# Routing weights of the first expert layer: spread by DMA from DRAM in fp32 instead of by a matmul of bf16 parts

## The reference

```python
scores = sigmoid(x @ gate_w.T)                      # 64 experts
rw = weights of the 8 chosen experts per token, 0 for all others   # [T, 64], fp32
expert_out = vmap(lambda gw, uw, dw: silu(x @ gw.T) * (x @ uw.T) @ dw.T)(Wg, Wu, Wd)
routed = einsum('eth,te->th', expert_out, rw)
shared = silu(x @ Sg.T) * (x @ Su.T) @ Sd.T
out = routed + shared
```

## Time and profile before

| | us |
|---|---|
| median of 3 runs (1984.31 to 1989.08) | 1984.51 |
| the profiled execution, whole time | 1989.54 |
| its span | 1987.7 |
| `setup` and `attention`, to about | 383 |
| `route0`, to | 493.7 |
| `block0`, from DVE's first L1594 to its last | 1014.4 |
| `block1` and the output, from 1509.6 | 478 |

### The profile page before, as it was taken

One profiled execution on the slowest core, in us unless ns is written; L12 is line 12 of the kernel. 1 busy time (PEld: TensorE's weight loads), 2 busy tenths in 40 slices (PEclk: granted clock), 3 DMA queues, 4 the chain that ended last, 5 costly groups with the idle time before them and its releaser, 6 DMA issues. The chain is left out here.

```text
span 1987.7 us, 25546 instructions
## 1 busy us (share of the span) xinstructions
PE 1782.0 (90%) x7668; PEld 1062.7 (53%) x7668; DVE 1425.5 (72%) x2688; ACT 809.7 (41%) x1501; POOL 677.8 (34%) x610
## 2 busy tenths in 40 slices
PE   2888898652999999999899899998998999999999
PEld 1455555351666656656566565565664455555555
DVE  5777777378666786986979969779699487444444
ACT  1466667532333324334343233342434443443333
POOL 2011111100000681945828638368194275000000
PEclk9989889855999999999999999999999999999999
DMA  7544444010223353333333333333330000000000
GB/s 267 151 134 111 120 119 115 23 51 13 104 106 111 101 178 94 99 90 97 89 95 98 87 95 95 90 100 85 95 101 11 1 6 6 6 6 5 6 5 5
DMA packets 101065, 157.68 MB, mean 79 GB/s; under 512 B 11077, under 2 KB 49310, under 8 KB 97785
## 3 DMA queue, kind: packets, MB, share of 16 engines
q1 hardware_dynamic: 97351, 154.61, 26.1%
q10 hardware_dynamic: 1586, 1.30, 0.2%
q0 software_dynamic: 2048, 0.79, 0.2%
HBM read 123.23 MB, written 33.42 MB: 79 GB/s over the span
## 5 line engine op out<-in xcount | busy, mean ns | idle before, releaser
L1296 PE MATMUL psum<-e_hhi,e_ring 128*128 128x512 f32 x704 | 478.2, 679 | 37.5 <-DVE e_hm L1737 26.2
L1551 ACT ACTIVATE e_gu<-psum 128x512 f32<-128x512 f32 (+1 forms) x368 | 219.1, 597 | 627.8 <-PE psum L1298 510.5
L1305 PE MATMUL psum<-e_hm,w_d 128*128 128x512 f32 (+1 forms) x736 | 378.6, 597 | 1.1 <-DVE e_hm L1733 1.1
L1733 DVE TENSOR_TENSOR e_gu<-psum,e_gu 128x512 f32<-128x512 f32 x352 | 240.9, 684 | 174.2 <-PE psum L1335 158.6
L1801 POOL TENSOR_TENSOR e_prod<-e_state,e_phi 128x512 f32<-128x512 f32 x256 | 355.3, 1424 | 5.5 <-DVE e_y L1608 3.2
L1769 DVE TENSOR_TENSOR e_hm<-psum,e_gu 128x512 f32<-128x512 f32 x256 | 175.2, 689 | 203.7 <-ACT e_gu L1576 152.0
L1297 PE MATMUL psum<-e_hhi,e_ring 128*128 128x512 f32 x704 | 281.2, 399 | 0.0
L1298 PE MATMUL psum<-e_hlo,e_ring 128*128 128x512 f32 x704 | 280.5, 399 | 0.0
L1415 PE MATMUL psum<-e_hm,w_gu 128*128 128x512 f32 x512 | 264.0, 601 | 3.2 <-DVE w_d L1751 2.6
L1576 ACT ACTIVATE e_gu<-psum 128x512 f32<-128x512 f32 x256 | 152.4, 597 | 279.0 <-PE psum L1298 264.8
L1737 DVE TENSOR_TENSOR e_hm<-psum,e_gu 128x512 f32<-128x512 f32 x352 | 243.5, 692 | 12.1
(11 more groups left out here) (237 smaller groups left out, 2404.7 us busy)
## 6 DMA issues: line engine op xcount, KB each, us to landing
e_ring<-w_split SPq DMA_DIRECT2D x308, 256.0 KB, 2.6
qk_parts<-at_part SPq DMA_DIRECT2D x96, 192.0 KB, 2.9
w_split<-e_ring SPq DMA_DIRECT2D x44, 256.0 KB, 2.0
at_qs<-qk_parts SPq DMA_DIRECT2D x16, 576.0 KB
at_ks<-qk_parts SPq DMA_DIRECT2D x16, 576.0 KB
w_gu<-in_w SPq DMA_DIRECT2D x2, 2048.0 KB, 10.4
sel_buf_r<-w_split SPq DMA_DIRECT2D x14, 256.0 KB, 2.6
w_gu<-in_wg SPq DMA_DIRECT2D x1, 2904.0 KB
```

Of the source, the lines that this page charges most:

```text
L1296: pe.matmul(out, w_hi, x_hi, start=first, stop=False)
L1305: mm = pe.matmul(ps[:, ACC, :], weights_at(T, WD + P * j, P)[0:rows(j), :], hm[0:rows(j), slot(j), :], start=(j == 0), stop=(j == HT - 1))
L1551: a(act_g[0:r, j % 2, :], ps[0:r, GB[j % 2], :], ACT.Silu).then_inc(silu_done, 1)
L1733: ins = v.tensor_tensor(product, ps[0:r, UB[j % 2], :], act_g[0:r, j % 2, :], ALU.mult)
```

## The change

`route0` no longer cuts the weights into bf16 parts. PE transposes `w1` itself in fp32 (32 transposes, 4 for each chunk), ACT and DVE copy 64 x 512 values for even and odd chunks, and SP writes them to a DRAM tensor `rw_dram` of 64 x 4096. All of it waits for these 8 writes.

In `block0` the spreading matmul and `sel` are gone. SP loads the weights of a tile's rows into one of four slots `rb` in SBUF: one DMA per expert that owns rows in the tile, with the expert's row of 2 KB read once for each hidden row (2 or 3 DMAs per tile, 104 per chunk). DVE multiplies up by the slot into bank RB, which is in PSUM, and then that by the silu. Only the second of these waits for the silu.

```diff
@@ route0: the parts
-            dve.wait_ge(weighted, 2)
-            for u in range(2):
-                dve.wait_ge(upper_cut, u + 1)
-                v.tensor_tensor(half(w0, u), half(w1, u), part(0, u), ALU.subtract).then_inc(rest_ready, 1)
...
-            with dve.Fori(0, CHUNKS // 2) as i:
-                keep(2 * i, 0)
-                keep(2 * i + 1, 1)
+            for c in range(1, CHUNKS, 2):
                 dve.wait_ge(tr_done, c + 1)
-                v.tensor_copy(T["rw"][0:PARTS * EHALF, 1, ds(c * CHUNK, CHUNK)], ps[0:PARTS * EHALF, 3 + 2 * (k % 2), :])\
-                    .then_inc(tr_kept[1], 1)
+                v.tensor_copy(cols(rw_fm, c)[0:EXPERTS], ps[0:EXPERTS, 2 + c % 4, :]).then_inc(tr_kept[1], 1)
@@ route0: PE
+            for c in range(CHUNKS):
+                pe.wait_ge(weighted, 1 + c // (CHUNKS // 2))
+                if c >= 4:
+
+                    pe.wait_ge(tr_kept[c % 2], c // 2 - 1)
+                for t in range(CT):
+                    mm = pe.transpose(ps[0:EXPERTS, 2 + c % 4, t * P:(t + 1) * P], w1[:, (CT * c + t) * EXPERTS:(CT * c + t + 1) * EXPERTS],
+                                      T["ident"][:])
                 mm.then_inc(tr_done, 1)
@@ route0: SP
+            for c in range(CHUNKS):
+                sp.wait_ge(tr_kept[c % 2], c // 2 + 1)
+                sp.dma_start(cols(T["rw_dram"], c), cols(rw_fm, c)[0:EXPERTS]).then_inc(rw_out, 16)
+            sp.wait_ge(rw_out, 16 * CHUNKS)
@@ experts: SP
+            def load_rb(c, j):
+
+                if j >= ROUTED_TILES:
+                    return
+                if c > 0 or j >= RB_SLOTS:
+                    sp.wait_ge(gu_done, ROUTED_TILES * c + j - RB_SLOTS + 1)
+                s = j % RB_SLOTS
+                for first, last, e in owners(j):
+                    sp.dma_start(rb[first:last, s, :], T["rw_dram"][e:e + 1, c * CHUNK:(c + 1) * CHUNK].broadcast_to([last - first, CHUNK]))\
+                        .then_inc(rb_in[s], 16)
...
                     sp.dma_start(w_slots[slot_of(j)].bitcast(F32), split[j]).then_inc(split_in[slot_of(j)], 16)
+                    load_rb(c, j)
@@ experts: PE
-                if j < ROUTED_TILES:
-                    mm = pe.matmul(ps[:, RB[j % 2], :], sel[0:PARTS * EHALF, j % HALF_TILES, :],
-                                   rw[0:PARTS * EHALF, j // HALF_TILES, ds(c * CHUNK, CHUNK)], start=True, stop=True)
                 mm.then_inc(ur_done, 1)
@@ experts: DVE
-                    dve.wait_ge(silu_done, g + 1)
                     dve.wait_ge(ur_done, g + 1)
-                    product = gu[0:r, j % 2, :] if j < ROUTED_TILES else hm[0:r, slot(j), :]
-                    ins = v.tensor_tensor(product, ps[0:r, UB[j % 2], :], act_g[0:r, j % 2, :], ALU.mult)
                     if j < ROUTED_TILES:
-                        ins.then_inc(gu_done, 1)
+                        s = j % RB_SLOTS
+                        dve.wait_ge(rb_in[s], 16 * rb_loads(s, ROUTED_TILES) * c + 16 * rb_loads(s, j + 1))
+                        v.tensor_tensor(ps[:, RB[j % 2], :], ps[0:r, UB[j % 2], :], rb[:, s, :], ALU.mult).then_inc(gu_done, 1)
+                        dve.wait_ge(silu_done, g + 1)
                         dve.wait_ge(gu_done, ROUTED_TILES * c + j + 1)
-                        v.tensor_tensor(hm[:, slot(j), :], ps[:, RB[j % 2], :], gu[:, j % 2, :], ALU.mult).then_inc(hm_done, 1)
+                        v.tensor_tensor(hm[:, slot(j), :], ps[:, RB[j % 2], :], act_g[:, j % 2, :], ALU.mult).then_inc(hm_done, 1)
```

More of the change, by code:

```diff
@@ L878, in _ @@
             run(pe, step_)
-            pe.wait_ge(cut, 1)
-            pe.wait_ge(T["ffn0_loaded"], 16 * FFN0_LOADS)
-            def turn(c, k):
-                if k >= 2:
-                    for g in range(2):
-                        pe.wait_ge(tr_kept[g], c - 1)
-                for g in range(2):
-                    for t in range(CT):
-                        mm = pe.matmul(ps[0:PARTS * EHALF, 2 + 2 * (k % 2) + g, t * P:(t + 1) * P],
-                                       parts[:, ds(CT * c + t, 1), g, :, :].rearrange("p o i e -> p (o i e)"), T["ident_bf"][:],
-                                       start=True, stop=True)
-                mm.then_inc(tr_done, 1)
-            turn(0, 0)
-            turn(1, 1)
-            pe.wait_ge(cut, 2)
-            with pe.Fori(1, CHUNKS // 2) as i:
-                turn(2 * i, 2)
-                turn(2 * i + 1, 3)
+            for c in range(CHUNKS):
[5 more added lines that the diff above has]
+                                      T["ident"][:])
+                mm.then_inc(tr_done, 1)
         @block.scalar
@@ L921, in _ @@
                 nc.scalar.activation(lg[:, over(u)], lg[:, over(u)], ACT.Sigmoid).then_inc(scored, 1)
-            for u in range(2):
-                act.wait_ge(weighted, u + 1)
-                nc.scalar.activation(part(0, u), half(w1, u), ACT.Copy).then_inc(upper_cut, 1)
-            for u in range(2):
-                act.wait_ge(rest_ready, u + 1)
-                nc.scalar.activation(part(1, u), half(w0, u), ACT.Copy).then_inc(upper_cut, 1)
-            def keep(c, k):
-                act.wait_ge(tr_done, c + 1)
-                nc.scalar.activation(T["rw"][0:PARTS * EHALF, 0, ds(c * CHUNK, CHUNK)], ps[0:PARTS * EHALF, 2 + 2 * (k % 2), :], ACT.Copy)\
-                    .then_inc(tr_kept[0], 1)
-            with act.Fori(0, CHUNKS // 2) as i:
-                keep(2 * i, 0)
-                keep(2 * i + 1, 1)
+            for c in range(0, CHUNKS, 2):
+                act.wait_ge(tr_done, c + 1)
+                nc.scalar.activation(cols(rw_fm, c)[0:EXPERTS], ps[0:EXPERTS, 2 + c % 4, :], ACT.Copy).then_inc(tr_kept[0], 1)
         @block.vector
@@ L1046 @@
 EARLY_LOADS = ("wqkv", "wo", "wr", "b_r1", "sel1")
-FFN0_LOADS = len(EARLY_LOADS) + 5
+FFN0_LOADS = len(EARLY_LOADS) + 4
 ROUTER_STEPS = 20
@@ L1057, with owners, rb_loads @@
 W_SLOTS = 5
+RB_SLOTS = 4
+def owners(j):
+    rows = range(P * j, P * (j + 1))
+    return [(max(HIDDEN * e, rows[0]) - rows[0], min(HIDDEN * (e + 1), rows[-1] + 1) - rows[0], e)
+            for e in range(rows[0] // HIDDEN, rows[-1] // HIDDEN + 1)]
+def rb_loads(slot, j):
+    return sum(len(owners(i)) for i in range(j) if i % RB_SLOTS == slot)
 def slot_of(j):
@@ L1145, in experts @@
         g1 = rw[:, 0, :]
+        rb = rw[:, 1, :].bitcast(F32).rearrange("p (s c) -> p s c", c=CHUNK)
         GB, UB, RB, ACC, SIDE = (0, 1), (2, 3), (4, 5), 6, 7
@@ L1190, in experts @@
         split_in = [sem(f"split_in{s}") for s in range(W_SLOTS)]
+        rb_in = [sem(f"rb_in{s}") for s in range(RB_SLOTS)]
         w1h_done, w1l_done = sem("w1h_done"), sem("w1l_done")
@@ L1274, in _ @@
                 sp.dma_start(split[j], w_slots[slot_of(j)].bitcast(F32)).then_inc(split_out[slot_of(j)], 16)
+                load_rb(0, j)
             for s in range(W_SLOTS):
@@ L1922, in layout @@
     a["wo"] = i["L1_attn_Wo"]
-    owner = (np.arange(HALF_TILES * P) // HIDDEN).reshape(HALF_TILES, P)
-    one_hot = (owner[None] == np.arange(EHALF)[:, None, None])
-    a["sel"] = f(np.tile(one_hot, (PARTS, 1, 1)).astype(bf16))
     a["wr"] = i["L1_ffn_router_w"]
```

27 lines of the change are left out of this document (6 added, 21 removed).

## The result

| | us | |
|---|---|---|
| before, median of 4 runs beside it | 1986.8 | 1984.3 to 1989.7 |
| after, median of 4 runs | 1958.9 | 1953.2 to 1963.6 |
| ratio | 0.9856 | 95% interval 0.9824 to 0.9889 |
| forecast | 1930 | 1913 to 1958 |

The change makes the kernel 1.4% faster: about 28 us, half of the 55 that I forecast, and 0.9 us outside my range. The profiled run of the changed kernel is its slowest (1963.63 us, span 1961.8); the spans differ by 25.9 us.

The account below looks back on a forecast made before the run. PE sets the pace in chunk 0 and up to tile 24 of late chunks, DVE behind it. Savings 6.8 + 10.2 + 7.5 + 30.6 = 55.1 us from 1989.5, less 5.0, give 1929.4, said as 1930; range 1913 to 1958.

Parts of the forecast that it names:

- The end of `route0`: Between the weights being ready and `experts`: fp32 transposes, last copy and store end earlier, saving 6.8 us.
- The spreading matmul's worth: In `block0`, each removed matmul frees 0.237 us where PE sets the pace; 22 count up to tile 24, giving 5.2.
- forecast 10.2: Chunk 0, where PE stays the bound: 43 x 0.237 = 10.2 us saved.
- The matmul in front of a projection: Tiles 12, 13 and 14 of chunks 2 to 7: removal gives nothing, and waits before the projections fall to about zero.
- Chunk 1: Chunk between the PE-bound and late ones: at least 5.2, at most 9.7 us saved, 7.5 taken.
- I take zero for all of it: Slot loads in `block0` cost nothing: DMA needs 1.86 of a tile's 2.26 us, and they are issued four tiles ahead.
- My forecast of a share of 0.67: Sign to look for in `block0`: DMA share near 0.67, no load waits on DVE or PE outside chunk 2's start.
- Same number, same kinds of input: DVE's multiplies in `block0`: the first, now writing PSUM, costs 0 to 0.31 us more; 0 taken.
- one drop per chunk: PE's clock in late chunks: one stretch at 0.57 for 4 us, after the 3.45 us wait before tile 43's up.
- a sign of failing: The prediction fails if PE's granted clock drops in more than one place of a chunk.
- My rival: TensorE loses its clock more often behind tile 24: up to 1.7 us per stretch, 24 in all, 1954; chance 0.10.

Follow-up runs that it names:

- experiment 12: Changed kernel with the silu wait before the first multiply, chunks 3 to 6 written out and only the first four slots loaded; 1928.3 us, ratio 0.9719.
- experiment 8: Changed kernel with the silu wait before the first multiply and chunks 3 to 6 written out; 1938.8 us, ratio 0.9751.
- experiment 7: Changed kernel with VectorE's silu wait moved from before the second multiply to before the first; 1948.9 us, ratio 0.9809.
- experiment 6: Changed kernel with only the first four slots loaded, plus a second, always satisfied wait before each first multiply; 1943.7 us.
- experiment 4: Changed kernel with a matmul of zeros on TensorE before the up matmuls of tiles 25 to 43 of chunks 2 to 7; 1961.0 us.
- experiment 1: Changed kernel with only the first four slots ever loaded, later tiles reading what stands in their slot; 1945.1 us, ratio 0.9779.

## Why the prediction was half right

- **The end of `route0`: right.** 6.8 forecast, 7.6 measured.
- **The spreading matmul's worth: right, with some luck.** From tile 23 on, the second multiplies of chunk 3 stand 5.2 to 5.5 us earlier than in chunk 5 before, where 22 x 0.237 = 5.2 was forecast. But 0.7 of it is there at tile 0 already, by the `e_hlo` multiply (0.69 us in place of 1.35); the matmuls gave about 4.6. In chunk 0 the run with the first four slots alone gained 10.5, forecast 10.2. The matmul in front of a projection did not quite vanish: the weight loads of three projections of chunk 3 wait 1.1 us in all, where I said zero, and the projections start 0.32 to 0.33 us behind the matmul ahead, where one stream takes 0.237.
- **Chunk 1: mis-sized.** I took 7.5 and called 5.2 the least. Without slot loads it gave 4.5 (5.1 in experiment 12), and no run says why.
- **"I take zero for all of it" (the slot loads): wrong, the first of the two steps that failed.** I had compared 1.86 us of DMA with 2.26 us of tile, and steady chunks bear that out. But chunks 0 and 1 are not steady. At the start of chunk 0 the slots' loads come with the first stores and nothing is ahead; at the start of chunk 1 five weight slots and the tiles' slots have to be filled at once, and an engine share of 0.80 leaves little to catch up with (that account is argued; the waits are in the rows above). Price by the chunks: 4.0 + 4.9 + 2.7 = 11.6 us, 10.8 between experiments 8 and 12; by the medians 1958.9 - 1945.1 = 13.8 and 1938.8 - 1928.3 = 10.5. My forecast of a share of 0.67 was near in chunks 2 to 7 (0.61 to 0.66); I never asked what it is in the chunks with the fastest tiles and the most to transfer, though the earlier trace rows had 0.29 and 0.41 there and the slot loads add some 0.4.
- **"Same number, same kinds of input" (VectorE's multiplies): wrong, the second.** Their time was right: the first took 693 ns on average after, 684 before. The Trainium skill, VectorE: DVE Perf Modes, first table, has VectorE closer to SBUF than to PSUM; on the output side this trace puts 9 ns on that at most, since the second multiply, which writes SBUF, takes 692 in both kernels. But I counted multiplies and not the semaphores that they wait for. In the written-out chunks the second multiply got a second one, 0.07 us on the path between two dependent instructions: 3.5 us of chunk 7 and 2.8 of chunk 2 (experiment 7), part of it in jobs that took longer behind it (experiment 8).
- **What I had no term for: the late start of chunks 4 to 6.** The three take 10.0 us more than three times chunk 3. 8.1 of them are there when the second multiply of tile 0 starts (7.33, 7.15 and 7.52 us into the chunk, 4.62 in chunk 3), 1.72 to 1.74 us behind a packet of instructions (experiment 6). Another 1.1 is lost in chunk 6 up to tile 10, most of it at the lower clock, and 0.8 at its end, also at the lower clock. Written out, the stall doesn't occur.
- **The clock: the count was wrong, the price in part.** I said one drop per chunk, two or three came, which the prediction had named as a sign of failing. My rival gave each up to 1.7 us. The additional one in the late tiles cost nothing (experiment 4), one behind the stall of chunk 6 about 0.8 (one case, read from the trace alone), and a long one at a chunk's end 0.7 to 1.2.

The account of `block0` against the forecast, in the profiled run: 3.7 in chunk 0, 8.0 in chunk 1, 3.6 in chunk 2, -0.6 in chunk 3, 8.9 in chunks 4 to 6, 3.4 in chunk 7, together 27.

Open: the profile doesn't name the engine whose instructions a packet carries, and no run shows why the kernel before, whose loop body is as long as that of experiment 1, fetches none at the start of chunks 4 to 6. Also open is how much of chunk 0 is the spread over the engines and how much SP's issuing.

## What to carry to other kernels

Count the waits of every instruction beside its operands when an edit rewires a chain, above all on a multiply that depends on the one ahead of it; moved before an instruction without such a dependence, the wait cost nothing here. A transfer that fits the average tile can still cost at the start of a stage, where buffers have to be filled at once, so compare the DMA share of the first stages and not that of the steady one. If an edit gives its forecast in one iteration and not in its copies, lay the iterations side by side tile by tile: the place where they part points at the cause that sums over lines hide, and among the queues of the profile look at that of the instructions too. Here that led to a version 2.5% faster than the kernel before, where the change alone gave 1.4%.
